# Switched attention, one core: the context products behind the fourth output unit, the norm a slot sooner

## The reference

```python
gate_v = sel_gate(x, sel_v_w, rs)      # sigmoid, the best 2 of 8 experts per head, normalised
gate_o = sel_gate(x, sel_o_w, rs)
q = einsum('bsd,hpd->bhsp', x, q_w);  k = einsum('bsd,hpd->bhsp', x, k_w)
xv = einsum('bsd,hedp->bshep', x, v_w)
v = einsum('bshep,bshe->bhsp', xv, gate_v)
att = softmax(einsum('bhqp,bhkp->bhqk', q, k) * SCALE)
ctx = einsum('bhqk,bhkp->bqhp', att, v)
out = einsum('bshep,hepd->bsd', ctx[:, :, :, None, :] * gate_o[..., None], o_w)
```

## Time and profile before

| what | value |
|---|---|
| time, median of 3 runs | 3278.0 us (3276.26 to 3281.53) |
| the profiled execution, its own time | 3283.84 us |
| its span in the trace | 3282.1 us |
| granted TensorE clock over the span | 0.923 of full |
| PE busy | 2945.8 us, 90% |
| PEld busy | 2215.6 us, 68% |
| DVE busy | 2780.9 us, 85% |
| ACT busy | 2342.4 us, 71% |
| POOL busy | 2319.9 us, 71% |

### The profile page before, as it was taken

The page is one execution under the profiler, slowest core; times in us unless marked ns, Lnnn a source line. Parts: engine busy times, 40 slices in busy tenths (PEclk is TensorE's granted clock), DMA queues, the critical chain, the costliest instruction groups (busy, mean ns, idle before and its releaser), DMA issues.

```text
span 3282.1 us, 78570 instructions
## 1 busy us (share of the span) xinstructions
PE 2945.8 (90%) x24633; PEld 2215.6 (68%) x24646; DVE 2780.9 (85%) x9101; ACT 2342.4 (71%) x7540; POOL 2319.9 (71%) x3111
## 2 busy tenths in 40 slices
PE   6639998289667999599999999999999999999998
PEld 5526775167435777477777777777777777777776
DVE  4369997599898998698898989898999889898987
ACT  3275665878796666477777777777777777777776
POOL 1179997565687666377777777777777777777777
PEclk7559998589678999799999999999999999999999
DMA  3000000022000110300000000000000000000000
GB/s 107 19 10 17 16 17 8 17 74 72 5 1 17 29 31 28 114 21 8 7 9 9 7 8 8 9 8 8 7 9 9 8 7 9 9 8 8 8 8 5
DMA packets 133086, 63.73 MB, mean 19 GB/s; under 512 B 20544, under 2 KB 132288, under 8 KB 132672
## 3 DMA queue, kind: packets, MB, share of 16 engines
q1 hardware_dynamic: 132672, 58.70, 6.3%
HBM read 41.82 MB, written 8.45 MB: 15 GB/s over the span
## 4 chain that ended last, share of the span: by engine, by line
PE 57%; ACT 1%; DVE 1%; POOL 0%; DMA 0%; issue 0%; SPq 0%; POOLq 0%; ACTq 0%; DVEq 0%
PE ps_sw_a L2173 23%; PE ps_sw_d L2173 21%; PE ps_sw_w L2219 4%; PE ps_sw_w L2206 3%; PE ps_sw_s L2188 2%; PE ps_sw_s L2230 2%; PE ps_sw_m L2195 1%; ACT sw_scaled L1914 0%; PE ps_sw_m L2181 0%; DVE sw_v_part L2069 0%; DMA sw_v<-in_L_ffn_v_w 0%; ACT sw_probs L1963 0%; DVE sw_v_low L2008 0%; ACT sw_v_high L1969 0%; PE ps_sw_w L2236 0%
## 5 line engine op out<-in xcount | busy, mean ns | idle before, releaser
L1914 ACT ACTIVATE sw_scaled<-ps_sw_a,sw_gate_o 128x128 f32<-128x128 f32 x2048 | 620.3, 447 | 254.1 <-PE ps_sw_a L2173 248.2
L1914 ACT ACTIVATE sw_scaled<-ps_sw_a,sw_gate_v 128x128 f32<-128x128 f32 x2048 | 597.4, 448 | 194.4 <-PE ps_sw_a L2173 192.7
L2069 DVE SCALAR_TENSOR_TENSOR sw_o_part<-ps_sw_d,sw_gate_o,sw_o_part 128x128 f32<-128x128 f32 x1920 | 554.9, 338 | 63.2 <-PE ps_sw_d L2173 60.5
L1841 POOL TENSOR_TENSOR sw_v_pair<-sw_v_part,sw_scaled 128x256 f32<-128x256 f32 x512 | 382.1, 746 | 156.0 <-DVE sw_v_part L2069 98.9
L2069 DVE SCALAR_TENSOR_TENSOR sw_v_part<-ps_sw_d,sw_gate_v,sw_scaled 128x128 f32<-128x128 f32 x1024 | 303.7, 337 | 122.1 <-PE ps_sw_d L2173 104.7
L1867 POOL TENSOR_TENSOR sw_o_rest<-sw_o_rest,sw_scaled 128x256 f32<-128x256 f32 x384 | 285.4, 743 | 157.9 <-ACT sw_scaled L1914 120.8
L2069 DVE SCALAR_TENSOR_TENSOR sw_v_part<-ps_sw_d,sw_gate_v,sw_v_part 128x128 f32<-128x128 f32 x1024 | 304.1, 337 | 0.0
L1870 POOL TENSOR_TENSOR sw_o_rest<-sw_o_rest,sw_scaled 128x256 f32<-128x256 f32 x384 | 282.6, 736 | 30.1
L1846 POOL TENSOR_TENSOR sw_v<-sw_v_pair 128x128 f32<-128x128 f32 x512 | 243.8, 476 | 40.1
L985 POOL TENSOR_TENSOR at_key_wide<-at_keyT,c_half_heads 128x1024 f32<-128x1024 f32 x128 | 242.6, 1895 | 4.2 <-ACT at_keyT L1082 4.2
L2173 PE MATMUL ps_sw_a<-sw_v_high,sw_xT_high 128*128 128x512 f32 x512 | 234.6, 458 | 8.2 <-DVE sw_v_low L2008 8.2
(11 more groups left out here) (337 smaller groups left out, 8584.4 us busy)
## 6 DMA issues: line engine op xcount, KB each, us to landing
at_ctxT<-ctx_T SPq DMA_DIRECT2D x128, 64.0 KB, 1.8
re_values<-in_ctx SPq DMA_DIRECT2D x128, 64.0 KB, 2.4
x<-in_x SPq DMA_DIRECT2D x16, 256.0 KB, 3.4
l_ctx<-in_ctx SPq DMA_DIRECT2D x16, 256.0 KB, 3.0
re_ctx<-in_ctx SPq DMA_DIRECT2D x16, 256.0 KB, 3.2
scratch_x<-x SPq DMA_DIRECT2D x64, 64.0 KB, 1.9
sw_x<-scratch_x SPq DMA_DIRECT2D x64, 64.0 KB, 1.9
sw_x_res<-scratch_x SPq DMA_DIRECT2D x64, 64.0 KB, 1.8
```

The source lines that it names most:

```text
L1841: pool.tensor_tensor(v_pair[:, h % 2], v_part[:, h], scaled[:, h % 4, 2:4], ALU.add)\
L1914: act.activation(scaled[:, h % 4, e], ps_a[h % 2][:, e], ACT.Copy, scale=gates[:, s, h, HALF_E + e:HALF_E + e + 1]).then_inc(a_scaled[kind ...
L2069: dve.scalar_tensor_tensor(out=acc[:, e % 2], in0=ps_d[h % 2][:, e], scalar=gates[:, s, h, e:e + 1], in1=before, op0=ALU.mult, op1=ALU.add ...
```

## The change

Four lists are reordered; no instruction is added, removed or resized.

- PE: `context` moves from behind unit o1 to behind unit o3.
- ACT: before, the o block was o0, o1, o2, keep_ctx(0), o3, exps 0, o4, keep_ctx(1), o5, exps 1, o6, exps 2, o7, exps 3. After, it is o0, o1, o2, exps 0, o3, exps 1, keep_ctx(0), o4, keep_ctx(1), exps 2, o5, exps 3, o6, o7. ("exps n" is `exp_scores` of two heads.)
- DVE: `norm` moves from the start of the iteration (lag 1) to behind half 1 of o2 of the iteration before (lag 0). The three `front` steps move from the o block to the v block, behind v2 half 1, v5 half 0 and v6 half 0. `peak` stands behind o1 half 0 (before: o1 half 1), `shifts` behind o1 half 1 (before: o2 half 0), and the routing pair R[15], R[16] behind o2 half 0 (before: o1 half 0). Some later routing steps shift by a place.
- POOL: `rstd` moves from between add_o(5) and add_o(6) to ahead of add_o(0).

```diff
@@ POOL
-                stages += [(3, add_o(h)) for h in range(6)] + [(0, rstd)] + [(3, add_o(h)) for h in range(6, SH)]
+                stages += [(0, rstd)] + [(3, add_o(h)) for h in range(SH)]
@@ ACT
-                stages += [(1, keep_u(0)), vs[6], (1, keep_u(1)), vs[7]] + os[:3] + [(2, keep_ctx(0)), os[3], exps[0]]
-                stages += [os[4], (2, keep_ctx(1)), os[5], exps[1], os[6], exps[2], os[7], exps[3]]
+                stages += [(1, keep_u(0)), vs[6], (1, keep_u(1)), vs[7]] + os[:3] + [exps[0], os[3], exps[1]]
+                stages += [(2, keep_ctx(0)), os[4], (2, keep_ctx(1)), exps[2], os[5], exps[3], *os[6:]]
@@ DVE
-                    "v": [[], [], [(2, sums(0))], [(2, sums(1))], [(2, sums(2))], [], *R[0:5], R[5] + R[6], R[7],
-                          R[8] + R[9], R[10], R[11]],
-                    "o": [R[12], R[13] + R[14], R[15] + R[16], [(1, peak)], [(1, shifts)], R[17], R[18],
-                          [(2, low_ctx(0))], [(0, front(0))], R[19] + [(0, front(1))], [(0, front(2))],
-                          [(2, low_ctx(1))], [], [], [], []],
+                    "v": [[], [], [(2, sums(0))], [(2, sums(1))], [(2, sums(2))], [(0, front(0))], *R[0:4],
+                          R[4] + [(0, front(1))], R[5] + R[6], R[7] + [(0, front(2))], R[8] + R[9], R[10], R[11]],
+                    "o": [R[12], R[13] + R[14], [(1, peak)], [(1, shifts)], R[15] + R[16], [(0, norm)], R[17],
+                          [(2, low_ctx(0))], R[18], [(2, low_ctx(1))], [], R[19], [], [], [], []],
                 }
-                stages = [(1, norm), (1, only_first(keep_pairs))]
+                stages = [(1, only_first(keep_pairs))]
@@ PE
-                stages += [vs[5], (1, pair_keys(1)), vs[6], vs[7], os[0], (1, scores), os[1], (2, context)]
-                stages += os[2:]
+                stages += [vs[5], (1, pair_keys(1)), vs[6], vs[7], os[0], (1, scores), *os[1:4], (2, context)]
+                stages += os[4:]
```

## The result

The changed kernel took 3323.3 us (median of 4 runs, 3320.4 to 3327.8) beside 3278.9 us for the kernel before on the same chip: a ratio of 1.0134, 95% interval 1.0122 to 1.0147, so 44 us more. The prediction was 3307 us, 29 more, in a range of 3266 to 3334. The direction and the place were right and the size was short. One execution of the last experiment's kernel took 9455 us and is in no ratio.

The account below looks back on a forecast made before the run. PE's list was taken to set the pace. Per tile 0.40 (DVE at o3) + 0.39 (ACT at the border) - 0.32 (old border wait) = 0.47 us, times 62 is 29 us on 3278: 3307 us, range 3266 to 3334.

Parts of the forecast that it names:

- The context's wait is not paid: PE ahead of the context matmuls: the wait for POOL's last v addition is worth only 0.01 us a tile.
- ACT at the border, 0.39 in place of 0.32: From o block to v block, PE's v0 load waits for ACT's o6: 0.39 us a tile, replacing 0.32 before.
- DVE ahead of o3's d bank, 0.40: PE's load for o3's d matmuls waits for DVE's mix of o1: 0.40 us a tile, bounds 0.25 and 0.71.
- The `front` steps come on top ... I take 0.10 together: In DVE's list ahead of o1's mix, `front(1)` and `front(2)` add 0.10 us together, bounds 0 and 0.34.
- Norm and `rstd`*: these are 0: DVE's norm behind o2 and POOL's `rstd` in idle time ahead of o1 neither gain nor cost anything: 0.
- The rival of `rstd`'s hold: POOL's running `rstd` holds DVE's R[13]: 3328 us (10%), or 3366 us if R[14] then loses to POOL's o1 addition (7%).
- The rival "no change": DVE reaches o1 about 0.4 us sooner, as moved POOL v additions block fewer routing steps: 3282 us, 15%.
- The rival "faster": The wait at v0's load, 0.32 us a tile, goes and no other comes: 3258 us, 13%.

Follow-up runs that it names:

- the last experiment's kernel: The kernel before with only ACT's list changed, exps 1 behind o6 and exps 2 and 3 behind o7: 3277.0 us beside 3280.0, ratio 0.9986.

## Why the prediction was right, and where it fell short

- **The context's wait is not paid.** Right: 0.37 before, 0.37 after, POOL or no POOL in the row.
- **ACT at the border, 0.39 in place of 0.32.** Right to the hundredth, and the lateness came where the exponents 2 and 3 stand ahead of o6; moving them gave 0.36 back. It showed at o7's a bank as well (0.10) as at v0 (0.29), which the working had put on one load; what PE waits at o7 it no longer waits at v0. The two waits behind it vanished as worked out.
- **DVE ahead of o3's d bank, 0.40.** The wait and its cause are right: the context's 1.93 us were DVE's time to read o1. It measured 0.58. The step that failed is "*The `front` steps come on top ... I take 0.10 together*": what came on top was about 0.3, inside the bounds of 0.25 to 0.71 for the whole term. The front steps were sized well enough: 0.13 by their starts. What was missing is that DVE's earlier list would change its durations.
- **"*Norm and `rstd`*: these are 0".** This is where it was missing. The line asked only whether `rstd` fits in its new place (it does, and it does not hold R[13]). It did not ask what its old place did: 0.55 of delay for POOL, by which the additions of the v block kept out of `route(0)`'s way. With it gone `route(0)` takes 0.31 more. A step of the same size in the old place took 15 us off, though it brought POOL's addition only 0.30 of the 0.73 back. The norm itself cost nothing, as said, while R[13] and R[14] stay where they are, and took 0.34 in place of 0.79.
- **The wait at o0's d bank, 0.06.** Not foreseen. It has the same root: DVE reads v6 out later. It went with POOL's delay given back.
- **The rival of `rstd`'s hold.** Refuted by R[13] at 0.28 beside a running `rstd`. The Trainium skill (SBUF — State Buffer, "SBUF: two separate sides") says whoever starts first on the shared port pair keeps it for the whole instruction; this trace agrees for POOL's addition on 128x256 (`route(0)`, 0.59) and disagrees for the power on 128x1 (R[13], 0.28).
- **The rival "no change".** It had the right mechanism with the wrong sign: POOL's additions in the v block did move and did block other routing steps, but the balance was 0.21 against DVE. Its "against" (blocked steps follow the additions that DVE's own mix starts, so they move along) fails for the additions that follow POOL's own backlog, as v2's does.
- **The rival "faster".** As a mechanism it was real, but it needs three more edits: two exponents later, `peak` and `shifts` later, `route(0)` later. Then it gives 3261 us, beside the 3258 it named. That is another kernel, so the nearness says that the border's wait was priced well, not that the rival was close here.
- **The whole.** 62 x (0.58 + 0.06 + 0.39 - 0.32) = 44 us against 29: all of the miss is DVE's.

What stays open: where the rest of POOL's shift in the v block comes from, and whether the hold depends on the operation or on its width; neither was tried alone.

## What to carry to other kernels

When a step is moved away from an engine, price its old place as well as its new one: what ran behind it now runs sooner, and may meet another engine's step that had been free. On DVE and POOL that meeting is worth up to 0.6 us for a step of 0.2, so look at each short DVE step on SBUF for the POOL step that will be running when it starts, and try it half a slot to either side. When two engines are late at the same place, relieving one of them may show almost nothing (here 3 us of 20); relieve both before judging.

## What the runs showed of the hardware that was not expected

- A DVE step with a single SBUF operand is held by POOL's addition just as one with two is: `route(0)` 0.23 to 0.59, `shifts` on 128x8 0.17 to 0.74, R[16] on 128x16 0.175 to 0.60. Where both rows stand above, it ends 0.09 and 0.02 behind POOL's. The length of the hold is POOL's, down to 8 elements a partition. The mixes, which read PSUM, keep their 0.60 a pair beside the same additions.
- In two cases here a step on 128x1 stands outside of this, one on either side. POOL's power on 128x1 (0.54) does not hold R[13], a step with two SBUF operands. And in the kernel before `front(2)`, on 128x1, runs wholly inside a POOL addition in 0.14, which is what it takes in the changed kernel beside an idle POOL (so in 61 of the 64 tiles):

```profile
2698.12 0.14 DVE L223 TENSOR_SCALAR sw_var<-sw_mv 128x1 f32<-128x1 f32 x1
```

```profile
2697.60 0.74 POOL L1870 TENSOR_TENSOR sw_o_rest<-sw_o_rest,sw_scaled 128x256 f32<-128x256 f32 x1
```

- An added POOL step of 0.55 that computes nothing made two kernels faster, by 15 and by 20 us.
